# One megakernel, two orders changed at once: patch loads on ScalarE's queue with split text loads, and values turned ahead of contexts

## The reference

```python
z = layernorm(patches) * g1 + b1            # 32 x 36 patches of 768
z = layernorm(z @ W_proj + b_proj) * g2 + b2
h = concat([cls, z], 1) + pos_emb           # 37 rows a sequence
h = concat([h, txt], 1)                     # 32 x 69 x 256
n = layernorm(h)                            # 16 heads of 64
h = h + softmax(q(n) k(n)^T / 8) v(n) @ l_w.T + l_b
n = layernorm(h)                            # 2208 tokens
h = h + moe(n)      # 8 experts, top 2 of n @ w_g, capacity 690, gelu(x @ c_fc) @ c_proj
```

## Time and profile before

| | us |
|---|---|
| median of 3 runs (726.61 to 731.09) | 730.72 |
| the profiled execution's own time | 728.92 |
| its span in the profile | 727.2 |
| PE busy / DVE busy / ACT busy / POOL busy | 693.2 / 506.7 / 291.5 / 281.3 |
| patch stage, up to the first qkv block | about 54 |
| attention, up to the last context | about 54 to 417 |
| router and first gather | about 417 to 450 |
| eight experts | about 450 to 727 |

### The profile page before, as it was taken

One profiled execution on the slowest core, in us unless ns is written; L12 is line 12 of the kernel. 1 busy time (PEld: TensorE's weight loads), 2 busy tenths in 40 slices (PEclk: granted clock), 3 DMA queues, 4 the chain that ended last, 5 costly groups with the idle time before them and its releaser, 6 DMA issues.

```text
span 727.2 us, 16884 instructions
## 1 busy us (share of the span) xinstructions
PE 693.2 (95%) x6651; PEld 653.0 (90%) x6651; DVE 506.7 (70%) x1143; ACT 291.5 (40%) x652; POOL 281.3 (39%) x294
## 2 busy tenths in 40 slices
PE   8699999999999999999999886999999999999995
PEld 6588899899898998989989886999999999999995
DVE  6687887878978789787877571747575665647471
ACT  4354544544444454444544221514343332425130
POOL 4564010030401304012030345365666666666706
PEclk9989999999999999999999897999999999999998
DMA  9651000000000000000000413343434535444202
GB/s 265 172 160 31 1 2 17 3 17 17 19 16 2 18 18 18 17 2 18 17 18 18 131 35 98 90 89 98 92 86 91 125 73 136 101 92 101 21 10 29
DMA packets 51521, 42.99 MB, mean 59 GB/s; under 512 B 25435, under 2 KB 45081, under 8 KB 51457
## 3 DMA queue, kind: packets, MB, share of 16 engines
q1 hardware_dynamic: 22289, 30.49, 13.8%
q0 software_dynamic: 29168, 11.61, 10.0%
HBM read 32.76 MB, written 10.25 MB: 59 GB/s over the span
## 4 chain that ended last, share of the span: by engine, by line
PE 67%; DVE 18%; issue 4%; SPq 4%; ACT 3%; DMA 2%; POOL 1%; POOLq 0%; DVEq 0%; ACTq 0%
PE pair L1420 11%; PE pair L1422 11%; PE pair L1421 11%; PE lone L1420 8%; PE lone L1421 7%; PE lone L1422 7%; PE pair L1538 3%; PE ct_ps L1548 3%; DVE zsum L1063 3%; DVE vals L1073 2%; DVE top L1054 2%; PE vt_ps L1525 2%; DVE expo L1057 2%; SPq L456 2%; ACT expo L826 1%
## 5 line engine op out<-in xcount | busy, mean ns | idle before, releaser
L768 POOL DMA_INDIRECT out<-yrow,held x48 | 100.9, 2102 | 74.7 <-DVE yrow L1382 60.6
L949 ACT ACTIVATE act_f<-pair 128x348 f32<-128x348 f32 (+1 forms) x128 | 51.8, 457 | 97.8 <-PE pair L1422 97.8
L1420 PE MATMUL pair<-xe_hi,fc_hi 128*128 128x348 f32 (+1 forms) x256 | 82.9, 324 | 1.1 <-DVE xe_lo L1363 1.1
L1422 PE MATMUL pair<-xe_hi,fc_lo 128*128 128x348 f32 (+1 forms) x256 | 83.2, 325 | 0.0
L1421 PE MATMUL pair<-xe_lo,fc_hi 128*128 128x348 f32 (+1 forms) x256 | 83.2, 325 | 0.0
L751 POOL DMA_INDIRECT held<-token_rows,found_ix x48 | 69.2, 1442 | 28.8 <-issue 21.9
L1420 PE MATMUL lone<-pj_hi,act_hi 128*116 128x256 f32 (+1 forms) x256 | 72.1, 282 | 0.0
L1422 PE MATMUL lone<-pj_hi,act_lo 128*116 128x256 f32 (+1 forms) x256 | 71.9, 281 | 0.0
L1421 PE MATMUL lone<-pj_lo,act_hi 128*116 128x256 f32 (+1 forms) x256 | 71.8, 280 | 0.0
L812 ACT ACTIVATE qkv<-lone,bq_sb 128x276 f32<-128x276 f32 x100 | 48.6, 486 | 55.8 <-PE lone L1422 55.8
L812 ACT ACTIVATE qkv<-pair,bq_sb 128x276 f32<-128x276 f32 x92 | 44.7, 486 | 55.0 <-PE pair L1422 55.0
(11 more groups left out here) (246 smaller groups left out, 1991.1 us busy)
## 6 DMA issues: line engine op xcount, KB each, us to landing
raw_fc<-c_fc SPq DMA_DIRECT2D x8, 1024.0 KB, 7.0
raw_pj<-c_proj SPq DMA_DIRECT2D x8, 1024.0 KB, 7.4
raw<-w_qkv SPq DMA_DIRECT2D x6, 512.0 KB, 7.6
raw<-patches SPq DMA_DIRECT2D x6, 384.0 KB, 4.9
out<-h SPq DMA_DIRECT2D x8, 276.0 KB
token_rows<-sent POOLq DMA_DIRECT2D x7, 285.7 KB, 7.2
qkv<-patches SPq DMA_DIRECT2D x3, 384.0 KB, 10.0
raw<-w_l SPq DMA_DIRECT2D x1, 1024.0 KB, 7.7
```

Of the source, the lines that this page charges most:

```text
L768: pool.indirect_dma_start(out, bass.IndirectOffsetOnAxis(ap=xg[p][0:n, t, D:D + 1].bitcast(U32), axis=0), yrow[p][0:n, t, :], None, bounds ...
L949: gelu = act.activation(act_f[f % 2][:, a:b], pair[f % 2][:, h, 0:b - a], ACT.Gelu)
L1420: pe.matmul(dst, l_hi, r_hi, start=(first and n == 0), stop=False)
L1422: done = pe.matmul(dst, l_lo, r_hi, start=False, stop=(last and n == len(terms) - 1))
```

## The change

It does six things.
1. Patches 5 to 8 are loaded from ACT's queue (`load_patch` in ACT's loop, iteration i loads i+5), and so is `w_l` (iteration 4). ACT splits weight pieces 3 to 5 one iteration later; POOL's low part of piece 3 moves into iteration 6.
2. SP's order: weight piece 3, then the texts of group 0 alone, piece 4, rows 0, piece 5, rows 1, text runs 0 and 1 of groups 1 to 7, rows 2, constants, text run 2, rows 3, text runs 3 and 4, then the other rows. POOL waits for the later texts (`s_texts`) ahead of `add_positions(1)`, which moves behind the patch loop.
3. In PE's unit `turn_values(m)` stands ahead of `context(m-1)`.
4. The previous group's steps move: projection halves in u 0 and 1, `turn_y` 2, `turn_x2` 4, logits 5, `count` in 6 behind the blocks; on DVE residual in 2, `norm_mid_end` in 3, picks in 5; on ACT the same shifts, `put_gap` in 6. The bank order follows. DVE's `put_place` is cut in two (`put_place`, `put_row`) and done in u 7 for the last group too.
5. `project_last` runs in the last two units (pairs 0 to 2, 3 to 5), then pair 6 behind the last context, six spares, pair 7; `tabulate(last, -2)` and four spares stand ahead of `turn_y`.
6. Expert 0 starts by halves: the first three gathered tiles are turned and expanded through all eight f while the others land (four f, turn the second half, four f); then `stage_d` expands the second half alone.

```diff
             load_wq(2)
...
-            load_patch(5)
             txt_seq = txt.rearrange("(g b) s d -> b s g d", b=BPG)
-            for b, n, r, t, m in TEXT_RUNS:
-                sp.dma_start(every[r:r + m, t, :, :], txt_seq[b, n:n + m, :, :]).then_inc(s_text, 16)
+            def load_text(run, groups, done):
+                b, n, r, t, m = run
+                sp.dma_start(every[r:r + m, t, groups, :], txt_seq[b, n:n + m, groups, :]).then_inc(done, 16)
+            load_wq(3)
+            for run in TEXT_RUNS:
+                load_text(run, slice(0, 1), s_text)
+            load_wq(4)
             move_rows(0)
-            load_wq(3)
-            load_patch(6)
-            load_wq(4)
+            load_wq(5)
             move_rows(1)
-            load_patch(7)
-            load_wq(5)
-            load_patch(8)
+            load_text(TEXT_RUNS[0], slice(1, GROUPS), s_texts)
+            load_text(TEXT_RUNS[1], slice(1, GROUPS), s_texts)
+            move_rows(2)
...
+            load_text(TEXT_RUNS[2], slice(1, GROUPS), s_texts)
+            move_rows(3)
+            for run in TEXT_RUNS[3:]:
+                load_text(run, slice(1, GROUPS), s_texts)
+            for i in range(4, PT - 1):
+                move_rows(i)
...
+            def load_patch(i):
+                act.wait_ge(s_pT, i - PBUF + 1)
+                act.wait_ge(s_a_ln, A_LN * (i - PBUF) + 1)
+                act.dma_start(patch[i % PBUF], patches[i]).then_inc(s_patch[i % PBUF], 16)
...
+                if i + PBUF < PT:
+                    load_patch(i + PBUF)
-                if i < 6:
+                if i < NOW:
                     high_wq(i)
+                if NOW < i <= 6:
+                    high_wq(i - 1)
+                if i == 4:
+                    act.dma_start(wl_raw, w_l.rearrange("(k p) n -> p k n", p=128)).then_inc(s_wll, 16)
...
+                turn_values(m)
                 if m >= 1:
                     context(Step((m - 1) // UNITS), (m - 1) % UNITS)
-                turn_values(m)
                 if m + 1 < ALL:
                     score(m + 1)
+                if u == 4 and before:
+                    turn_x2(st, -1)
                 if u == 5 and before:
-                    turn_x2(st, -1)
-                if u == 6 and before:
                     logit(st, -1, "x2t", x2T, wg_sb)
-                if u == 7 and before:
-                    count(st, -1)
+                if m == ALL - 2:
+                    project_last(range(3))
+                if m == ALL - 1:
+                    project_last(range(3, 6))
                 if blocks:
...
-                if u == 3 and before:
+                if u == 2 and before:
                     turn_y(st, -1)
...
+                if u == 6 and before:
+                    count(st, -1)
-                if u in (0, 2) and before:
-                    project_out(g - 1, u // 2)
+                if u in (0, 1) and before:
+                    project_out(g - 1, u)
...
-            project_last(range(4))
             context(Step(GROUPS - 1), UNITS - 1)
-            project_last(range(4, UNITS - 1))
-            project_last(range(UNITS - 1, UNITS))
+            project_last(range(UNITS - 2, UNITS - 1))
             pe.wait_ge(s_sub, ALL)
             spare(6)
+            project_last(range(UNITS - 1, UNITS))
+            tabulate(last, -2)
+            spare(4)
             turn_y(last, -1)
             logit(last, -1, "proj", yT, wg_mid)
-            tabulate(last, -2)
             spare(20)
...
+            turn_first(0)
+            pe.wait_ge(s_xe_lo, KD)
+            pe.wait_ge(s_fc_lo, 4)
+            for f in range(EARLY):
+                expand_first(f)
+            turn_first(1)
+            for f in range(EARLY, KF):
+                expand_first(f)
```

More of the change, by code:

```diff
@@ L167, in bank_uses @@
         order += unit_uses(m)
[L168 to L169 removed]
+    order += [("table", last - 1, 0), ("ytr", last, 0), ("ytr", last, 1), ("logit", last, 0), ("rank", last, 0),
+              ("table", last, 0)]
     return {use: (n % BANKS, n // BANKS + 1) for n, use in enumerate(order)}
@@ L418, in load_patch @@
             def load_patch(i):
[L419 to L422, removed]
+                sp.dma_start(patch[i], patches[i]).then_inc(s_patch[i], 16)
             def load_wq(n):
@@ L941, in _, with put_first, first_gelu @@
                 split_fc(Step(0), 0, q)
-            put_xe(Step(0), 0)
+            def put_first(h):
+                a, b = HALVES[h]
+                for c in range(KD):
+                    act.wait_ge(s_xe, KD * h + c + 1)
+                    act.activation(xe_hi[:, c, a:b], (vt_ps, ct_ps)[c][:, 0:b - a], ACT.Copy).then_inc(s_xe_hi, 1)
+            def first_gelu(f):
+                a, b = HALVES[0]
+                act.wait_ge(s_half_mid, f + 1)
+                if f >= 2:
+                    act.wait_ge(s_half_lo, f - 1)
+                act.activation(act_f[f % 2][:, a:b], pair[f % 2][:, 0, 0:b - a], ACT.Gelu).then_inc(s_half_gelu, 1)
+            put_first(0)
+            for f in range(EARLY):
+                first_gelu(f)
+            put_first(1)
+            for f in range(EARLY, KF):
+                first_gelu(f)
             def stage_d(st):
+                first = st.i == 0 and st.k is None
                 for f in range(KF):
@@ L947, in stage_d @@
                     wait(act, s_act_lo, st, lambda i: KF * i + f - 1)
-                    for h, (a, b) in enumerate(HALVES):
+                    if first and f < 2:
+                        act.wait_ge(s_half_lo, KF - 1 + f)
+                    for h, (a, b) in list(enumerate(HALVES))[first:]:
                         gelu = act.activation(act_f[f % 2][:, a:b], pair[f % 2][:, h, 0:b - a], ACT.Gelu)
@@ L1306, in unit @@
                     pick(st, -1, 1)
-                if u == 7 and before and more:
+                if u == 7 and before:
                     put_place(st, -1)
+                    put_row(st, -1)
             for m in range(ALL):
@@ L1745, in multiply, with expand, expand_first @@
                              first=blocks[0] == 0, last=blocks[-1] == KF - 1)
+            def expand(f, h):
+                a, b = HALVES[h]
+                w = slice(f * 128, (f + 1) * 128)
+                return three(pair[f % 2][:, h, 0:b - a],
+                             [(fc_hi[:, k, w], fc_lo[:, k, w], xe_hi[:, k, a:b], xe_lo[:, k, a:b]) for k in range(KD)])
+            def expand_first(f):
+                if f >= 2:
+                    pe.wait_ge(s_half_gelu, f - 1)
+                expand(f, 0).then_inc(s_half_mid, 1)
+            turn_first(0)
+            pe.wait_ge(s_xe_lo, KD)
+            pe.wait_ge(s_fc_lo, 4)
+            for f in range(EARLY):
+                expand_first(f)
+            turn_first(1)
+            for f in range(EARLY, KF):
+                expand_first(f)
             def stage_d(st):
+                first = st.i == 0 and st.k is None
                 wait(pe, s_xe_lo, st, lambda i: 2 * KD * (i + 1))
@@ L1753, in stage_d @@
                         wait(pe, s_yrow, st, lambda i: XT * i - 2)
-                    w = slice(f * 128, (f + 1) * 128)
-                    for h, (a, b) in enumerate(HALVES):
-                        done = three(pair[f % 2][:, h, 0:b - a],
-                                     [(fc_hi[:, k, w], fc_lo[:, k, w], xe_hi[:, k, a:b], xe_lo[:, k, a:b]) for k in range(KD)])
+                    for h in range(first, 2):
+                        done = expand(f, h)
                     done.then_inc(s_mid, 1)
                 wait(pe, s_pj_lo, st, lambda i: 4 * (i + 1))
+                if first:
+                    pe.wait_ge(s_half_lo, KF)
                 for t in range(2):
```

89 lines of the change are left out of this document (62 added, 27 removed).

## The result

Medians: the changed kernel **722.72 us** (720.52 to 723.72), the kernel before 729.32 (726.61 to 731.09), six runs each. Ratio 0.9908, 95% interval 0.989 to 0.9926. The profiled spans are 721.3 and 727.2, so 5.9 us are to be found; the forecast had 14.8.

A forecast was written before the change was run, and what follows sets the result against it. The prediction took PE to set the time, with DVE nearly the bound; head -5.0, group 0 -0.4, groups 1 to 6 -2.5, last group -0.5 and expert -6.4 sum to -14.8, forecast 715.5 us, range 706 to 722.

The forecast's parts named there:

- -5.2 + 0.2 for POOL = -5.0: Head: earlier loads close the patch-stage hole, less a stall and POOL's slowing of DVE; 5.0 us saved, bounds -1.5 and -9.
- about 1.1 us of stall: Head: `norm_z(8)` waits for rows 4, queued behind the 161 text rows and landing at about 50.3; about 1.1 us.
- rival B: Head: SP stops behind the run of 23 partitions, rows 4 land 4 to 5 us later; about 720, chance 0.10.
- 0.42 a group, 2.5: Groups 1 to 6: period 44.9 to 45.0 against 45.36, most of PE's saving waited away; 2.5 us saved.
- 0.15 a unit: PE's units: values ahead of contexts cost 1.29 us in change-overs instead of 1.44; 0.15 saved, bounds 0 and 0.3.
- VectorE is the bound: Groups: DVE is nearly the bound, so most of what PE saves is waited away in u 6 and 7.
- Rival A: Groups: DVE has slack and PE's order pays in full, 13.5 less; about 702, half of it 709; chance 0.16.
- rival C: Units: DVE waits in `low_ctx` for the later context in each unit, 26 us more; 741, chance 0.05.
- 0.4: Group 0: DVE sets the time up to unit 4, so the change saves 0.4 us there.
- -0.5: Last group: `turn_y` only 1.6 us sooner after a `tabulate` wait, low clock takes 1.1 back; bounds +2 and -5.4.
- -6.4: First expert: starting by halves ends at 461.75 instead of 468.19, clock taken as full; bounds -3.5 and -7.
- Rival D: Head: patches on ACT's queue land late and DVE waits for them, 5 us back; 721, chance 0.07.

The follow-up runs named there:

- rows ahead: Changed kernel with SyncE storing the rows of tile 4 before it issues the two late text runs; 717.03 us, ratio 0.9855 to the kernel before.
- run cut: Changed kernel with the late text run of 23 partitions issued as one of 16 and one of 7, same place; 716.59 us, ratio 0.983.
- table behind: Changed kernel with the last but one table product put behind the last logits again instead of ahead of the last turning; 718.94 us, ratio 0.9878.
- picks apart: Changed kernel with VectorE's second pick moved from unit 5 to 6 and the count to ahead of unit 7's blocks; 719.64 us, ratio 0.9877.
- three mends: Changed kernel with tile 4's rows before late texts, second pick and count a unit later, last but one table product behind last logits; 708.28 us, ratio 0.9712.
- the head alone: Kernel before with only the changed loads (patches and w_l on ScalarE's queue, text runs split, weight pieces earlier); 729.38 us, ratio 1.0013.
- contexts first: Changed kernel with the contexts ahead of the values in each unit again, all else as changed; 719.70 us, ratio 0.9882 to the kernel before.
- these with contexts first: The kernel with the three mends, with the contexts ahead of the values again; 707.71 us, ratio 0.9708 to the kernel before.
- expert alone: Kernel before with only the first expert's first half of tokens turned and expanded for eight blocks before the second half; 723.62 us, ratio 0.9935.
- count amid: Kernel with the three mends, and the count of unit 7 between its second and third block instead of ahead of the first; 705.86 us, ratio 0.9678.
- VectorE held up: Fastest kernel (three mends, count amid the blocks) with two scratch reductions added to VectorE behind the first pick; 720.94 us, ratio 0.9899.

## Why the prediction was wrong, point by point

**The step that failed: the head, "-5.2 + 0.2 for POOL = -5.0", in its term "about 1.1 us of stall".** The rest of that step held. VectorE's work did follow directly: `project(8)` moved by 6.6 us (up to 6.3 forecast), and without the stall the first values come 6.4 us sooner than before (rows ahead; run cut 6.6). The stall measured 4.11 us, and by what remains the slow clock behind it took the rest, some 2.4. (In table behind, where the clock was low for 3.4 us less, the first values came 1.6 us sooner.) The 1.1 came from letting the transfer of 161 rows run from 41.3 and queueing the rows of tile 4 behind it, as if SyncE went on issuing. It doesn't: the next issue stood for 3.32 us, as one had for 11.14 of the 12.82 us in the earlier trace rows. The stop makes the rows of tile 4 be issued 2.6 us later than with the run cut (45.90 against 43.26), and they landed 2.6 us later than forecast (52.9 against 50.3); VectorE was ready 0.3 sooner (48.94 against 49.2). The remainder, the 1.1, is what the forecast had. Why the next issue stands still behind a run on few engines, no run shows.

I wrote this down as rival B, priced it (about 720) and gave it 0.10, with "that stop had a full backlog ahead" against it. The backlog wasn't needed: a run of 7 x 23 did it with the DMA engines at a share of 0.05. B left out the head's slow clock, though the hole of the earlier trace rows had brought the same 6.8 us of it. That 722.7 lies only 3 us above B's 720, as much as the clock cost in two groups, is partly luck: group 0 (0.7) and the expert (1.6) gave too little, the last group 1.7 too much, and these nearly cancel.

**Groups 1 to 6, "0.42 a group, 2.5": the mechanism right, the clock missing.** The forecast waits are there: `turn_x2` 0.25 to 0.29 (0.3), none at the count, 1.1 at the values of unit 7 (1.0), scores 0.2 late behind it (0.3), and an undisturbed period of 44.8 to 45.1 (44.9 to 45.0). At full clock the six periods would sum to 2.2 us less than before. What came on top is 1.5 us in each of two groups, for a clock that never fell in the groups before. The prediction listed the waits as waits only.

**Values first, "0.15 a unit".** A plain unit is 4.21 to 4.22 against 4.36, and contexts to scores need 0.64, as assumed. But the 0.42 was not this order's own: with the old steps it gives 0.50 a group (44.86), with the new steps nothing (45.02 with either), with picks apart 0.13. And the new steps with the old order give 0.34 (45.02). With either half alone TensorE already waits for VectorE in unit 7 (0.95 at the count, 0.58 at the contexts), so the second half finds nothing left. Without the new order the changed kernel measured 0.9882 against 0.9908. The intervals overlap, and the difference is the low clock of two groups and of the expert in the profiles, so whether the order makes the kernel slower isn't shown.

**VectorE is the bound.** Right, and shown from both sides: 1.41 us more in its unit 5 lengthen the period by 1.4; one pick less in unit 5 shortens it by 0.6. Rival A (702 to 709) and rival C (741) fall: the periods of groups 2 to 6 lay between 44.8 and 45.1 at full clock. What neither rival saw is that the load of VectorE lies unevenly in a group: the kernel with three mends runs the same instructions as the changed one, in another order.

**Group 0, "0.4".** Wrong by 0.7: +0.3. TensorE waits 0.8 us at the values of unit 3 and 1.1 at those of unit 6. The first of these waits belongs to the head: it is absent, and the group 0.4 us shorter (36.53 and 36.54), in rows ahead and in run cut, where SyncE's stop doesn't hold the rows up, and the head alone lengthens the old group by as much (37.70 against 37.31 from values to values). The other 0.3 was not followed up.

**Last group, "-0.5".** -2.2. From the start of group 7 the turning is 2.7 us sooner (1.6 forecast). The wait at the table product was 2.05 and not 3.8: TensorE's work ahead of it gained 4.8 and not 5.4, and by the rest of the sum GpSimd's spread was ready 1.1 us sooner than reckoned, for a reason that was not followed up. The low clock of 6.8 us behind the wait came, but what was lost later is 0.5 and not 1.1. Table behind shows that the place itself, with its clock, costs 2.7 us. So this term erred to the good side, by 1.7.

**First expert, "-6.4": the size right at full clock.** From gathered tokens to multiplication there are two values in the eleven profiles with the halves, one apart: 18.8 (rows ahead, contexts first, table behind, three mends, and these with contexts first) when the clock stays full, which is 25.17 less 6.36; and 20.3 to 20.4 (changed, expert alone, picks apart, run cut, count amid) when it is 0.5 for 3.4 us. VectorE held up, with 6.8 us of it, took 21.2. "I take the clock as full" was the flaw: in six of the eleven profiles it wasn't.

**Rival D** (patches late) fell: after the first patch, at the start, no engine waits for one, and the hole is closed.

By the Trainium skill, "DMA: Bandwidth & Descriptors", "Why a DMA increments its semaphore by 16 and not by 1", a run of 23 partitions goes to one engine, and its parts of 16 and 7 to 16 and 7. The traces agree: a DMA share of 0.05, about one engine of 16, behind the run of 23, and 0.41 us an issue instead of a stop of 3.3 when it is cut. The Trainium skill's section "Issuing engines are not separate DMA queues" on the same page spoke for rival D, and by it the change of queue wins nothing by bandwidth. The head alone gave nothing, though for another reason, and no run here tests that rule.

## What to carry to other kernels

When a queue is reordered, give each issue its own duration in the old trace and look for the one behind which the queue stood: its cost moves with it and lands on whatever is issued next. When two edits both spare TensorE time and TensorE already waits for VectorE, cost them together, not one by one. Then look for the one heavy step of VectorE to move rather than for a cheaper order of matmuls: splitting two picks over two units was worth 0.62 us a group, the new order at best 0.50. A wait of a microsecond on TensorE has a second price, the clock, and it comes only some of the time, so a forecast needs it as a case with a chance.

## What the runs showed of the hardware that was not expected

- A wait of 1.1 us of TensorE, in work that is dense on both sides, was followed by 3.4 us at 1.2 instead of 2.4 GHz in 7 of 32 places (group 0 counted), one of 1.65 us in 4 of 6, waits up to 0.95 in none of 54 groups. Among short matmuls an idle time of 0.79 us was followed by it once. What decides which place is hit is open.
- The issue behind a text run of 161 rows on 23 partitions stood for 3.3 us with the DMA engines at a share of 0.05; with the run cut into 16 and 7 partitions, the same rows cost 0.41 us an issue.
- After a wait of 4.6 us of TensorE the clock stayed low for 6.8 us, after one of 3.9 in the same place (table behind) for 3.4, after one of 3.7 (picks apart) for 6.8: the length of the wait alone doesn't tell.
